# Keys and values of the last attention computed for all tiles during the MLP, its queries by pairs, one written-out order for every engine

## What is computed

```python
# block 0 (first attention and MLP)
q = layernorm(x) @ Wq;  k, v = layernorm(ctx) @ Wkv
x = x + softmax(q k^T / 4) v @ Wproj + bproj
x = x + gelu(layernorm(x) @ W1 + b1) @ W2 + b2          # 256 -> 1024 -> 256
# block 1 (last attention)
q = (x * rsqrt(mean(x*x) + eps) * norm_w) @ wq          # context goes in as it is
k, v = ctx @ wkv
q, k = rotate(q), rotate(k)                             # cos and sin by token
q, k = q / max(|q|, 1e-12), k / max(|k|, 1e-12)         # per head
out = x + softmax(4 q k^T) v @ wout
```

## Time and profile before

| | |
|---|---|
| device time, median of 3 runs | 389.51 us |
| span of the profiled execution, first to last instruction | 386.9 us |
| TensorE matmul, weight loads busy | 356.5 us (92%), 318.7 us (82%) |
| VectorE, ScalarE, GpSimd busy | 294.4, 239.3, 197.1 us |
| granted TensorE clock, mean | 0.999 of full speed |

### The profile page before, as it was taken

One profiled execution on the slowest core, in us unless ns is written; L12 is line 12 of the kernel. 1 busy time (PEld: TensorE's weight loads), 2 busy tenths in 40 slices (PEclk: granted clock), 3 DMA queues, 4 the chain that ended last, 5 costly groups with the idle time before them and its releaser, 6 DMA issues.

```text
span 386.9 us, 11499 instructions
## 1 busy us (share of the span) xinstructions
PE 356.5 (92%) x4475; PEld 318.7 (82%) x4475; DVE 294.4 (76%) x654; ACT 239.3 (62%) x464; POOL 197.1 (51%) x177
## 2 busy tenths in 40 slices
PE   8998999999999989898999999978889989989974
PEld 5977888888888867798999998978778878878854
DVE  4799987989899773267755559467899999999752
ACT  2356677666677655815644476163877777777862
POOL 2474544554665611003331233248899998999810
PEclk9999999999999999999999999999999999999999
DMA  6853001110000000000000000000001001010001
GB/s 157 246 158 121 27 25 43 32 28 25 2 3 4 22 2 2 2 2 0 0 0 0 0 0 3 10 22 0 22 12 36 26 26 42 29 37 14 29 30 41
DMA packets 14432, 12.39 MB, mean 32 GB/s; under 512 B 2996, under 2 KB 13752, under 8 KB 14392
## 3 DMA queue, kind: packets, MB, share of 16 engines
q1 hardware_dynamic: 14384, 11.83, 10.4%
q10 hardware_dynamic: 8, 0.00, 0.0%
HBM read 9.73 MB, written 2.10 MB: 31 GB/s over the span
## 4 chain that ended last, share of the span: by engine, by line
PE 58%; issue 22%; DVE 10%; ACT 5%; POOL 4%; POOLq 0%; DVEq 0%; ACTq 0%
PE bank_qk L697 9%; PE banks_s L745 6%; PE bank_y L834 4%; PE bank_y L828 3%; PE banks_s L1032 3%; PE bank_t L800 3%; PE bank_qk L722 3%; PE bank_o L736 3%; PE bank_t L697 3%; PE bank_qk L726 3%; DVE row_max L1203 2%; POOL x_all L375 2%; PE bank_y L1052 2%; PE bank_o L1021 2%; PE bank_y L929 1%
## 5 line engine op out<-in xcount | busy, mean ns | idle before, releaser
L413 POOL TENSOR_TENSOR norm_inv<-norm_sq_min,minus_half 128x32 f32<-128x32 f32 x16 | 87.5, 5468 | 1.8 <-DVE norm_sq_min L1374 1.8
L576 ACT ACTIVATE W_s<-banks_s,b_cols 128x256 f32<-128x256 f32 x60 | 25.0, 469 | 41.3 <-PE banks_s L915 41.3
L342 POOL TENSOR_TENSOR masked<-qkT_r,halves_t 128x512 fp32r<-128x512 f32 x32 | 32.9, 1050 | 24.1 <-DVE qkT_r L1193 24.1
L477 ACT ACTIVATE PT<-banks_s 128x1024 f32<-128x1024 f32 x32 | 31.0, 1022 | 20.3 <-PE banks_s L782 18.3
L1203 DVE TENSOR_REDUCE row_max<-banks_s 128x8 f32<-128x1024 f32 x32 | 37.6, 1218 | 7.7 <-PE banks_s L745 7.7
L368 POOL TENSOR_TENSOR b_var_eps<-b_mean_var,eps_t 128x2 f32<-128x2 f32 x8 | 1.6, 197 | 69.1 <-DVE b_mean_var L1137 69.1
L915 PE MATMUL banks_s<-lnT_hi,W_hi 128*128 128x256 f32 x120 | 34.2, 285 | 0.0
L915 PE MATMUL banks_s<-lnT_hi,W_lo 128*128 128x256 f32 x120 | 33.9, 283 | 0.0
L915 PE MATMUL banks_s<-lnT_lo,W_hi 128*128 128x256 f32 x120 | 33.9, 283 | 0.0
L642 ACT ACTIVATE PT<-banks_s 128x1024 f32<-128x1024 f32 x32 | 31.1, 1024 | 4.1 <-PE banks_s L1032 4.1
L745 PE MATMUL banks_s<-masked,qkT_r 32*128 32x256 f32 x768 | 31.5, 294 | 1.6 <-DVE row_max L1203 1.3
(11 more groups left out here) (171 smaller groups left out, 1095.6 us busy)
## 6 DMA issues: line engine op xcount, KB each, us to landing
ctx_in<-in_ctx SPq DMA_DIRECT2D x32, 96.0 KB, 2.0
x_all<-in_x SPq DMA_DIRECT2D x16, 128.0 KB, 2.1
W_s<-in_L_xattn_W SPq DMA_DIRECT2D x2, 1024.0 KB, 6.4
out<-Wq_s SPq DMA_DIRECT2D x16, 128.0 KB, 1.8
Wq_s<-in_L_xattn_Wq SPq DMA_DIRECT2D x1, 256.0 KB, 3.0
Wkv_s<-in_L_xattn_Wkv SPq DMA_DIRECT2D x1, 256.0 KB, 3.2
Wproj_s<-in_L_xattn_Wproj SPq DMA_DIRECT2D x1, 256.0 KB, 4.2
wout_s<-in_L_xattn_wout SPq DMA_DIRECT2D x1, 256.0 KB, 3.0
```

Source lines behind the costliest of these rows:

```text
L342: nc.gpsimd.tensor_tensor(masked[:, r, 1, :, half, :], qkT_r[:, r, 1, :, :].bitcast(fp32), ones, ALU.mult)\
L413: nc.gpsimd.tensor_tensor(norm_inv[:, j, :], norm_sq_min[:, j, :], minus_half[:, :], ALU.pow)\
L477: nc.scalar.activation(PT[:, 2 * h:2 * h + 2, :], banks_s[:, 2 * h:2 * h + 2, :], ACT.Exp, scale=HD ** -0.5)\
L576: last = nc.scalar.activation(hT[:, m, :], (bank or bank_s[u])[:, 256 * k:256 * k + 256], ACT.Gelu, bias=b1_cols[:, m:m + 1])
```

## The change

- Keys and values of block 1 (`keys_values`): 6 split products of 512 columns a tile, keys in the first 256 columns, values in the last. The stationary side is the context already turned: the host passes `ctx_T`, SyncE loads it a pair at a time, and GpSimd makes its halves (`context_hi`, `context_lo`). `inputs_c` turns only x.
- Keys of all tiles stay in `keysT` (fp32), values in `vals_c`. Both lie in SBUF room that the first attention's buffers had (`first` is closed before they are allocated). Keys go by pairs from rotation to transposition (`keys_turned` to `keys_out`), with norms on GpSimd (`keys_norms`).
- Queries go by pairs, on x not normalised. Since a query is divided by its own norm, the factor of the row falls out; it comes back in the clamp only: the sum is clamped at (mean(x*x) + eps) times 1e-24, made by `mean_square` and `clamp_c`.
- Scores are 8 whole fp32 products of 256 columns instead of 24 split ones; the queries' and keys' low halves are gone.
- The residual is added into `x_all`, which is stored; `y_out` is gone.
- `ln3_rows` and `b_xn` get rooms of their own. The splits of wkv move to GpSimd in the first attention (`split_wkv`), those of wq and wout are spread over pairs 0 and 1. `clamp_eps` and the two memsets of ctx_in rows are new.
- From the end of the first attention on there are no loops: each engine has one list of calls over both stages, and a part is given its bank as an argument (`up_b` no longer owns banks_s, `down_b` no longer bank_o and bank_y). TensorE's waits for a bank stand between the calls.

Core of the diff:

```diff
-            with pe.Fori(0, NP - 3) as i:
-                up_b(i + 1, True)
-                turn_b(i + 2)
-                down_b(i + 1, True)
+            def keys_values(t, bank):
+                pe.wait_ge(c_ctx_lo, t // 2 + 1)
+                for k in range(2):
+                    for n, (a, b) in enumerate(HI_LO):
+                        last = mm(bank[:, :], ctxT_r[:, a, k, in_pair(t % 2, TOK)], wkv_r[:, b, k, :], start=k == n == 0,
+                                  stop=k == 1 and n == 2)
+                last.then_inc(c_kv, 1)
+            def keys_T(p, bank):
+                pe.wait_ge(c_kunit, p + 1)
+                turned_pair(bank, rot_k).then_inc(c_kT, 1)
+            def inputs_c(p, bank):
+                pe.wait_ge(b_x, 2 * p + 2)
+                turned_pair(bank, x_all[:, in_pair(p, 2), :].rearrange("p b c -> p (b c)")).then_inc(c_xT, 1)
+            def queries_c(p, bank):
+                pe.wait_ge(c_x_lo, p + 1)
+                for j in range(2):
+                    last = split_mm(bank[:, in_pair(j, C1)], x_r[:, :, :, in_pair(j, TOK)], wq_r[:, :, :, :])
+                last.then_inc(c_q, 1)
+            def scores_c(t):
+                p, j = t // 2, t % 2
+                pe.wait_ge(c_masked, 2 * p + 2)
+                pe.wait_ge(c_keys, p + 1)
+                for k in range(KT):
+                    for g in range(NG):
+                        last = mm(bank_s[g][:, in_pair(k, 2 * TOK)], keysT[quad(g), k, in_pair(t, TOK)],
+                                  masked_q[quad(g), p % 2, k, :, in_pair(j, TOK)], start=True, stop=True)
...
+            def context_lo(p):
+                r = p % 2
+                pool.wait_ge(c_ctx_hi, p + 1)
+                nc.gpsimd.tensor_tensor(ctxT_r[:, 1], ctx_in[:, 2 * r:2 * r + 2, :], ctxT_r[:, 0].bitcast(fp32), ALU.subtract)\
+                    .then_inc(c_ctx_lo, 1)
+            def keys_norms(p):
+                pool.wait_ge(c_kmin, p + 1)
+                wait(pool, c_kunit, p)
+                nc.gpsimd.tensor_tensor(norm_k_inv[:, :], norm_k_min[:, :], minus_half[:, :], ALU.pow).then_inc(c_kinv, 1)
...
+            def exps_c(t):
+                act.wait_ge(C["scores"], NG * t + NG)
+                wait(act, C["av"], t)
+                for h in range(2):
+                    nc.scalar.activation(PT[:, 2 * h:2 * h + 2, :], banks_s[:, 2 * h:2 * h + 2, :], ACT.Exp, scale=HD ** 0.5)\
+                        .then_inc(C["exped"], 1)
```

More of the change, by code:

```diff
@@ L55 @@
 QUARTERS = 4
[L58 to L59 removed]
 def ok(tile):
[L64 removed]
+    return 0 <= tile < NB
 def wait(eng, sem, count):
[L69 removed]
+    if count > 0:
         eng.wait_ge(sem, count)
 def upto(tile):
[L75 to L90 removed]
+    return min(tile, NB)
 def build(nc, x, ctx, ln1_w, ln1_b, ln2_w, ln2_b, ln3_w, ln3_b, Wq, Wkv, Wproj, bproj, W1, b1, W2, b2,
[L94 removed]
+          norm_w, wq, wkv, wout, ctx_T, rope, halves, picks, out):
     es = ExitStack()
@@ L545, in _ @@
             step_a(NB)
-            lnT_b(0, False)
+            lnT_b(0, bank_t)
             exps_a(NB - 3)
@@ new lines, in queries_squares, with queries_out @@
+            def queries_squares(p):
+                act.wait_ge(c_qadd, p + 1)
+                wait(act, c_qsum, p)
+                nc.scalar.activation(sq_q[:, :], rot_q[:, p % 2, :], ACT.Square).then_inc(c_qsq, 1)
+            def queries_out(p, bank):
+                act.wait_ge(c_qT, p + 1)
+                wait(act, C["scores"], NG * (2 * p - 2))
+                for half in range(2):
+                    nc.scalar.activation(masked_q[:, p % 2, :, half, :], joined(bank[:, :]), ACT.Copy, scale=halves_t[:, half:half + 1])\
+                        .then_inc(c_masked, 1)
@@ L1286, in _ @@
             heads_a(NB - 1)
+            for u in range(3):
+                hidden_lo(0, u)
             residual_a(NB - 1)
[L1289 to L1299 removed]
```

1617 lines of the change are left out of this document (1135 added, 482 removed).

## The result

Five runs of the changed kernel gave a median of 371.67 us (368.79 to 372.10), against a median of 389.46 of the kernel before on the same chip. The ratio is 0.956, 95% interval 0.951 to 0.961: faster by 4.4%. The prediction said 369.3 us, 361 to 380. The profiled execution has a span of 366.9 us and took 368.79 us, where 366.7 us of span were predicted. That the span looks exact is luck: errors of 3 us stand against an early start of 3 us, as will be seen.

The account below looks back on a forecast made before the run. TensorE's weight loads were taken to bound the MLP, the exps round the last attention. 163.5 + 131.3 + 2.4 = 297.2, plus 69.5 gives 366.7 us of span; with 2.6 from span to time, 369.3 us, range 361 to 380.

Parts of the forecast that it names:

- the rival on the other side: Scores in both stages: whole fp32 products on row strips don't overlap, 3.56 us a step, 412 us in all; 5%.
- the term that ruled it out: Scores step: fp32 products on four row strips overlap, as the weighted values do on column strips; 0.89 us a tile.
- MLP stage: From 163.5 us to the last down product: 131.3 us of TensorE work plus 2.4 of waits, ending at 297.2.
- The three named ones: TensorE waits in the MLP stage: first keys and values 0.8 us, first weighted values 1.1, second wait for query masks 0.4.
- the margin of 0.4 us for key units: Plain MLP pair: key units follow at 5.3 us and TensorE wants them at 5.7, the thinnest margin.
- TensorE waiting on key units: MLP stage: listed among the signs that the prediction is wrong.
- the powers come late: Rival for the MLP stage: the key units' margin goes negative through context passes, adding 11 us, 380 us; 12%.
- the contention term: GpSimd passes slow VectorE, 1.07 us for two; sixteen context passes would cost 8.6 us, taken as covered.
- The walked chain: Plain MLP pair: a key pair's power ends 4.2 us in, units follow at 5.3, TensorE wants them at 5.7.
- Last stage: Attention left behind the MLP, tiles 3 to 15: 4.5 + 56.0 + 9.0 = 69.5 us.
- The ring: Short rounds of the last attention: exps, weighted values, scores wait in turn through PT's one buffer; 4.2 us.
- The long ones: Every second round of the last attention while queries are made, with extra ScalarE work ahead of exps: 5.6 us.

Follow-up runs that it names:

- Experiment 10: Changed kernel with all eight score products of a tile reading the first strip of 32 rows: 426.04 us (one run).
- Experiment 4: Changed kernel with GpSimd's two bias passes behind the small passes for the second to fifth pair: median 370.07 us against 371.95, MLP stage 132.9 us.
- experiment 12: Changed kernel with keys and values from high halves alone and GpSimd's pass for the context's low halves left out: MLP stage 127.0 us.
- experiment 2: Changed kernel with keys and values from high halves alone, 2 products a tile instead of 6: MLP stage 131.7 us.
- experiment 11: Changed kernel with two more transposes of a constant ahead of each tile's keys and values: median 372.21 us, MLP stage 136.6 us.
- experiment 3: Changed kernel with one more VectorE pass of 512 columns between each pair's power and key units: MLP stage 139.7 us.
- experiment 6: Changed kernel with a second buffer for the exponentials alone, order of all queues kept: rounds 4.37 us, last stage 69.3 us.
- experiment 7: Changed kernel with second buffers and a new TensorE order from tile 11 on: median 372.66 us, last stage 69.7 us.
- experiment 9: Changed kernel with later GpSimd biases, second buffers and a new order of the last tiles, mended in three places: median 367.29 us, 0.945 of the kernel before.
- experiment 1: The changed kernel run again with nothing edited: median 371.95 us over six runs.
- experiment 5: Changed kernel with the eight score products of a tile issued strip after strip: 0.76 us of loads a step, rounds 4.42 us.

## Why the prediction held, and where it was off

**Scores.** Four fp32 strips overlap: 0.74 us of loads, and 1.29 until the exps start, for 0.89 + 0.33 = 1.22 predicted. Experiment 10 shows that it is overlap and what it is worth: without it the kernel took 426 us (one run), so the rival on the other side was a real one (412 predicted), and the term that ruled it out was right.

**MLP stage.** 134.5 us for 133.7, by two errors that nearly cancel. The work was less, 134.5 - 5.6 = 128.9 us for 131.3. Of that, 1.1 us is known: six products of 512 columns take 1.37 us a tile (1.26 from 211.95 to the next load at 213.21, and the load after that comes 0.11 late), not 1.44. The waits were more: those of 0.3 us and above add up to 5.6 us for the 2.4 predicted. The three named ones came as said (0.64 at the first keys, 1.23 at the first weighted values, 0.35 at the masks and scores), but the margin of 0.4 us for key units was negative, by 0.36, 0.49, 0.67 and 0.83 us in four pairs: TensorE waiting on key units, which the prediction had named as a sign of being wrong. So the rival "the powers come late" took place, at 2.4 us and not 11. The step that failed is the contention term: it was charged to sums of engines ("it is covered") and not to the one chain whose margin was 0.4 us. The walked chain had 1.1 us for the units (4.2 to 5.3), nearly the 1.22 they took. What it lacked is the slower sum of the turned keys ahead of the power, 1.35 to 1.69 us beside the context pass for 0.69. In the pair shown (turn at 202.97) the power ends 5.1 us into the pair for 4.2, the units end at 6.3 for 5.3, and TensorE asks for them at 5.9 for 5.7. Experiment 4 takes away the other slowing, that of the units, by 0.53 us a pair, and that is enough to bring the chain nearly on time. Taking the context pass away was tried only with fewer products (experiment 12), so its own share of the waits isn't isolated. GpSimd's list was undersized too, 104.4 us for 96. What I called TensorE-bound is better called bound twice. Less work for TensorE brings 2.8 of 13 us (experiment 2), more costs 2.1 of 3.4 (experiment 11), a pass in the chain costs 5.2 (experiment 3).

**Last stage.** 69.9 us for 69.5: exps of tile 3 end 4.8 us behind the MLP (4.5), those of tile 15 end 55.4 later (56.0), and 9.65 us of tail (9.0; 9.1 in experiment 6, the rest is the lower clock of the last projection). The ring was sized 0.17 short in each short round (4.37 for 4.2: the weighted values start 0.11 us behind the exps for 0.07, the exps 1.29 behind the scores for 1.22, and 4.26 had been rounded down). While queries are made, rounds are 4.96 and 4.64 us in turn, for 5.6 and 4.2. The long ones were oversized because I summed single durations: the two masks take 1.28 us together for 1.44, and ScalarE's instructions in a row start before the one ahead ends, so that 3.5 us of them fit into the 3.02 between two exps. The others were undersized because the queries' products, 1.48 us, stand ahead of the weighted values. Its reason was half right: the ring is exps, weighted values, scores, but TensorE's order closes it, not the single buffer (experiment 6). The buffer matters once the order is turned: one wait left over from it was part of what made a round of experiment 7 6.1 us long, which takes 3.75 in experiment 9.

**First attention.** Here the prediction failed outright: "weight splits for keys and values move to GpSimd in the first attention ... where it has over 4 free: nothing". From the first exps to the handover it takes 134.56 us; before it took 132.58 (table of stretches of the kernel before):

```profile
30.95:163.53 132.58, 127.68 (x1982) 109.50 (x1983) 104.73 (x235) 91.36 (x159) 58.86 (x78) 1.00 0.09 25
```

GpSimd had the room, but VectorE's short copies of the maxima stand in TensorE's way, and they end when a GpSimd pass ends. VectorE's and GpSimd's timelines, first of the changed kernel, then of the kernel before at the same step:

```profile
117.51 1.40 DVE L1783 CAST max_cols<-row_max 128x16 fp32r<-128x16 f32 x1
117.60 1.27 POOL L410 TENSOR_TENSOR W_lo<-W_s,W_hi 128x512 fp32r<-128x512 f32 x1
```

```profile
120.25 0.26 DVE L1209 CAST max_cols<-row_max 128x16 fp32r<-128x16 f32 x1
119.21 1.27 POOL L386 TENSOR_TENSOR W_lo<-W_s,W_hi 128x512 fp32r<-128x512 f32 x1
```

The copy of 16 columns took 1.40 us and ended at 118.91, the pass at 118.87; before, it began as the pass was ending (120.48) and took 0.26. One step later it takes 1.81 us for 1.06, and VectorE has the two new memsets there, 0.55 us; one step earlier it is 1.76 for 0.73. These are 1.03 + 1.14 + 0.75 + 0.55 = 3.5 us on VectorE, of which 2.0 arrive at the handover: rounds of 8.56, 9.78 and 9.08 us in place of 8.33, 8.72 and 8.32. The passes of line 410 were there before (line 386); what is new are the splits of wkv ahead of them, 0.39 and 0.72 us, which push them onto the copies. This is read from the traces; no run put the splits back.

**The sum.** At the start that the kernel before had, the changed kernel's span would be 366.9 + 2.9 = 369.8 us. That is 3.1 over the prediction: 2.0 first attention, 0.8 MLP stage, 0.4 last stage (each rounded). The distance from span to time is 1.9 us in this run (368.79 less 366.9) and not 2.6, so 371.7 us, which is the median. The gain by like starts is 386.9 less 369.8, 17.1 us, where 20.2 were predicted. So 366.9 beside 366.7 is an early start of 2.9 us against 3.1 us of errors, all on the same side.

## What to carry over

When work is moved onto a nearly free engine, look for the chain with the least margin that runs beside it or shares a queue with it, not for free time in the sum; splits of 0.4 and 0.7 us that nobody waits for seem to have cost 2 us here, by pushing a longer pass beside a copy of 16 columns. A buffer that seems to set a round may only repeat what the order of a queue already says: give it a second copy on paper first, and see which wait ends last then. Compare stages by their lengths from a common event, since two profiled executions can differ by several us at the start alone, and check that a clock of 1.00 comes from a record and not from the lack of one: the price of a known instruction tells.

## What the runs showed of the hardware

- TensorE starts an execution at half speed: a transpose takes 0.204 us in the first fourteen and 0.108 later (the rows in experiment 1). It leaves that state at 4.4 to 4.9 us in three traces of the changed kernels and at 10.8 to 14.0 in ten, and the difference stays to the end. The granted clock reads 1.00 all the while, as the trace has no record of it before that moment.
- A short VectorE instruction (16 columns) can last as long as the GpSimd pass beside it. Of the copies of the maxima and the instruction that follows each (0.17 us alone), seven in the changed kernel and three before took over 0.4 us, and all ten ended within 0.1 us of the end of a GpSimd pass (118.91 and 118.87, 129.11 and 129.02 in the changed kernel; 130.04 and 130.01 before). The twelve other traces have seven each, with no exception. The Trainium skill (Advanced Engine Details and Errata, VectorE Performance Modes) notes that GpSimd instructions and VectorE's two-port ones "will interfere/block eachother"; the copy's 1.40 for 0.26 us agree, if it runs in such a mode, which no row shows.
- Whole fp32 products on four strips of rows overlap 4.5 to 1 in their loads (3.31 us on one strip against 0.74 on four), and do so in either order of issue (experiment 5: 0.76 us).
- After TensorE had stood for 2.16 us (experiment 2) or 0.59 and 1.02 us in a tail with little work (the changed kernel), its granted clock fell to 0.50, for some 3 us in the one and to the end in the other; with a wait of 1.23 us in the midst of full work (286.40 us in the changed kernel) it stayed at 1.00. The wait alone doesn't decide it: the same 2.16 us at the same place in experiment 12, and the same 0.59 and 1.02 us in the tail of experiment 6, left it at 1.00.
